# Cross attention 3's output projection and gate for its first eight token tiles, moved from the router's block into the attention's last iterations

## The reference

```
def _L1_xattn_ref(q, k, v, Wq, bq, Wk, bk, Wv, bv, Wo, bo):    # 16 heads of 16, 64 context rows
    ...
    attn = jax.nn.softmax(scores, axis=-1)
    out = jnp.einsum('bhqk,bhkd->bhqd', attn, vh)
    concat = out.transpose(0, 2, 1, 3).reshape(B, LQ, D_MODEL)
    return concat @ Wo + bo
x = x + jnp.tanh(g_xattn[1]) * _L1_xattn_ref(_layernorm(x, axis=-1), ctx_512, ctx_512, ...)
x = x + jnp.tanh(g_ffn[1]) * _L1_ffn_ref(_layernorm(x, axis=-1), ...)   # router, top 128 tokens of each of 16 experts, MLP, scatter
```

## Time and profile before

| | |
|---|---|
| median of 3 runs | 1970.08 us (1968.18 to 1970.22) |
| the profiled execution: its own time, its span | 1972.5 us, 1970.7 us |
| mean granted TensorE clock | 0.969 |
| block of cross attention 3, from the first normalisation to the last copy | 1674.0 to 1756.4 us |
| router's block up to the first MAX8 | 1757.2 to 1788.6 us |

### The profile page before, as it was taken

The page is one execution under the profiler, slowest core; times in us unless marked ns, Lnnn a source line. Parts: engine busy times, 40 slices in busy tenths (PEclk is TensorE's granted clock), DMA queues, the critical chain, the costliest instruction groups (busy, mean ns, idle before and its releaser), DMA issues. The chain is left out here.

```text
span 1970.7 us, 32332 instructions
## 1 busy us (share of the span) xinstructions
PE 1787.6 (91%) x11430; PEld 1165.9 (59%) x11430; DVE 1284.4 (65%) x2762; ACT 1034.9 (53%) x2194; POOL 693.5 (35%) x995
## 2 busy tenths in 40 slices
PE   6989999999899999998899989999999999882697
PEld 3445555555576666766567665557776555551696
DVE  5579999999724477232799973259999353878311
ACT  3479999999712345221677751147776211551232
POOL 0023333333324434242555551125556220360343
PEclk9989999999999999999899999999999999996899
DMA  3451111110000020020100002010000000037495
GB/s 123 130 172 44 44 44 44 44 44 2 2 0 1 1 60 1 1 66 0 47 5 5 4 6 71 0 47 15 7 7 6 6 0 1 17 115 185 135 321 148
DMA packets 102959, 97.23 MB, mean 49 GB/s; under 512 B 37056, under 2 KB 86544, under 8 KB 102672
## 3 DMA queue, kind: packets, MB, share of 16 engines
q1 hardware_dynamic: 99216, 90.84, 15.3%
q0 software_dynamic: 3584, 4.33, 1.2%
HBM read 78.23 MB, written 14.81 MB: 47 GB/s over the span
## 5 line engine op out<-in xcount | busy, mean ns | idle before, releaser
L613 DVE TENSOR_REDUCE negmax<-sps 128x1 f32<-128x1024 f32 x256 | 308.9, 1217 | 18.9 <-PE sps L535 14.4
L657 ACT ACTIVATE prob<-sps,negmax 128x1024 f32<-128x1024 f32 x256 | 285.5, 1116 | 25.3 <-DVE negmax L613 20.9
L1987 POOL TENSOR_TENSOR la_pr_x3kblk<-la_pr_x3kblk,la_ri 128x512 f32<-128x512 f32 x128 | 158.5, 1267 | 152.4 <-DVE la_ri L2086 152.4
L703 POOL TENSOR_TENSOR probT<-probT,after 128x128 f32<-128x128 f32 x256 | 116.9, 457 | 240.4 <-DVE probT L621 214.5
L2315 ACT ACTIVATE la_pr_x3kblk<-la_pr_x3kblk,la_nx 128x256 f32<-128x256 f32 x256 | 126.3, 494 | 100.9 <-DVE la_nx L2127 100.9
L535 PE MATMUL sps<-ks,qs 128*128 128x512 f16 x512 | 170.9, 386 | 7.6 <-PEq L42 3.1
L2537 PE MATMUL la_bs<-lf_zT,lfw 128*128 128x512 f32 x352 | 153.4, 594 | 0.0
L551 PE MATMUL tps<-ident,prob 128*128 128x128 f32 x704 | 126.1, 283 | 22.9 <-DVE probT L621 20.4
L551 PEld LDWEIGHTS tps<-ident,prob 128*128 128x128 f32 x704 | 80.6, 142 | 89.6 <-issue 44.0
L1997 POOL TENSOR_TENSOR la_qs<-la_qn,ores 128x256 f32<-128x256 f32 x128 | 97.1, 790 | 78.1 <-DVE la_qn L2143 78.1
L1614 PE MATMUL tx_s<-t_zT,tw 128*128 128x512 f32 x256 | 113.8, 593 | 1.3 <-ACT t_zT L1481 1.3
(11 more groups left out here) (384 smaller groups left out, 3867.4 us busy)
## 6 DMA issues: line engine op xcount, KB each, us to landing
w1e<-in_fc_T SPq DMA_DIRECT2D x16, 1024.0 KB, 6.2
w2e<-in_fc_T SPq DMA_DIRECT2D x16, 1024.0 KB, 9.3
qs<-q_parts SPq DMA_DIRECT2D x128, 64.0 KB, 1.9
ks<-k_parts SPq DMA_DIRECT2D x128, 64.0 KB, 1.9
q_parts<-parts SPq DMA_DIRECT2D x8, 512.0 KB, 3.6
k_parts<-parts SPq DMA_DIRECT2D x8, 512.0 KB, 3.6
tw<-in_L_xattn_a_li_w SPq DMA_DIRECT2D x4, 1024.0 KB, 8.2
lfw<-in_L_ffn_w SPq DMA_DIRECT2D x6, 640.0 KB
```

The costliest lines, as they stand in the source:

```text
L613: dve.tensor_reduce(negmax[:, n % 4:n % 4 + 1], slots[n % NS][:], X, ALU.max, negate=True).then_inc(s.max_done, 1)
L657: act.activation(prob[:, n % 3, :], slots[n % NS][:], ACT.Exp, bias=negmax[:, n % 4:n % 4 + 1], accum_out=rowsum[:, tile % 2, n % QUAD:n % ...
L703: pool.tensor_tensor(blk, blk, after[:], ALU.mult).then_inc(s.masked, 1)
L1987: ins = pool.tensor_tensor(prob[:, h:h + 2, :], prob[:, h:h + 2, :], rinv[:, h:h + 2].unsqueeze(2).to_broadcast([P, 2, 2 * P]), ALU.mult)
```

## The change

Eight of the sixteen tiles' projections leave the router's block. Inside the attention's block, TensorE gets `project_out(t)`, t = 0..7: two fp32 matmuls of 256 columns (four records in the profile), at the end of iterations 7 to 12 and, for tiles 6 and 7, ahead of `turn_probs(14, 0)` and `turn_probs(15, 0)`. They write the PSUM banks `zps` and `qps`, free by then. ScalarE gets `output_share(t)`, which copies such a bank times the gate into `share_of` (two buffers), at the end of its iterations 7 to 12, 14 and 15. GpSimd gets, at the block's start, the product gate times bias and eight additions of it to `xres` (`base`), and after `share(8)` to `share(15)` the eight additions of `share_of` (`advance`). The router's block keeps groups 2 and 3 of `project`, `base` and VectorE's addition; its statistics cover all four groups as before.

```diff
@@ cross_attention @@
-        def cross_attention(phase, H, DK, src, res, weights, context, biases, scale, ahead):
+        def cross_attention(phase, H, DK, src, res, weights, context, following, biases, scale, ahead):
...
+            wo, bo, gbo, carried, loads = following
+                share_of = sb(phase + "share", [P, 2, D], F32, c)
...
                     def _(pool):
...
+                        def base(t):
+                            pool.wait_ge(s.z_done, t + 1)
+                            pool.tensor_tensor(src(t), src(t), gbo[:], ALU.add).then_inc(s.base_done, 1)
+
+                        def advance(t):
+                            pool.wait_ge(s.base_done, t + 1)
+                            pool.wait_ge(s.w_out, t + 1)
+                            pool.tensor_tensor(src(t), src(t), share_of[:, t % 2, :], ALU.add).then_inc(s.advanced, 1)
+
+                        pool.wait_ge(s.next_in, loads)
+                        pool.tensor_scalar(gbo[:], bo[:], gate[:, 1:2], None, ALU.mult).then_inc(s.gbo_done, 1)
+                        pool.wait_ge(s.gbo_done, 1)
+                        for t in range(carried):
+                            base(t)
                         for t in range(ready, LEAD_X + AHEAD):
                             inverse_deviation(t)
                         for t in range(NT):
                             share(t)
+                            if 8 <= t < 8 + carried:
+                                advance(t - 8)
...
+                        def output_share(t):
+                            act.wait_ge(s.w_done, t + 1)
+                            if t >= 2:
+                                act.wait_ge(s.advanced, t - 1)
+                            act.activation(share_of[:, t % 2, :], (qps if t % 2 else zps)[:, 0:D], ACT.Copy,
+                                           scale=gate[:, 1:2]).then_inc(s.w_out, 1)
...
                                 queries(it + LEAD_Q)
+                            if 7 <= it < 13:
+                                output_share(it - 7)
+                            if it in (14, 15):
+                                output_share(it - 8)
...
+                        def project_out(t):
+                            if t == 0:
+                                pe.wait_ge(s.xT_done, NT)
+                                pe.wait_ge(s.next_in, loads)
+                            if t == 1:
+                                pe.wait_ge(s.qT_done, G * MC)
+                            pe.wait_ge(s.out_done, t + 1)
+                            if t >= 2:
+                                pe.wait_ge(s.w_out, t - 1)
+                            at = t % TPB * P
+                            for k in range(MC):
+                                mm = pe.matmul((qps if t % 2 else zps)[:, 0:D], res[:, t // TPB * MC + k, at:at + P], wo[:, k, :],
+                                               start=(k == 0), stop=(k == MC - 1))
+                            mm.then_inc(s.w_done, 1)
...
                                 weigh(it - 1)
+                            if 7 <= it < 13:
+                                project_out(it - 7)
...
                             weigh(t)
+                        project_out(6)
                         turn_probs(NT - 2, 0)
                         turn_probs(NT - 2, 1)
+                        project_out(7)
                         turn_probs(NT - 1, 0)
@@ router @@
+        CARRIED = 8
+        FIRST = CARRIED // J
...
-                    pool.wait_ge(s.gbo_done, 1)
-                    base(0)
+                    base(FIRST)
                     for i in range(2):
                         pool.memset(lane[i][:, 0:CAP // 2], 0.0).then_inc(s.zeroed, 1)
-                    base(1)
+                    base(FIRST + 1)
                     for g in range(G):
                         coefficients(g)
-                        if g + 2 < G:
-                            base(g + 2)
...
-                        for j in range(J):
+                        for j in range(J if g >= FIRST else 0):
...
-                    dve.tensor_scalar(gbo[:], bo[:], gate[:, 1:2], None, ALU.mult).then_inc(s.gbo_done, 1)
                     advance(0)
...
-                        if g >= 2:
-                            pe.wait_ge(s.x_done, (g - 1) * J)
...
-                    project(0)
-                    project(1)
-                    project(2)
+                    project(FIRST)
+                    project(FIRST + 1)
                     turn_rows(0)
                     for g in range(G):
                         route(g)
-                        if g == 0:
-                            project(3)
```

More of the change, by code:

```diff
@@ L739, in cross_attention @@
                 tps = ps(phase + "t_ps", [P, 512], c)
-                s = signals(phase, "@next_in @x_stats @x_moments @x_var "
+                s = signals(phase, "@next_in @gbo_done @base_done @w_done @w_out @advanced @x_stats @x_moments @x_var "
                             "@x_rstd @z_done @z_turned @xT_done @q_done @qT_done @scores @max_done @prob_ready @exp_done "
@@ L784, in _ @@
                     def _(sp):
-                        sp.wait_ge(s.next_in, ahead(sp, s.next_in))
+                        assert ahead(sp, s.next_in) == loads
+                        sp.wait_ge(s.next_in, loads)
                     @block.gpsimd
@@ L2619, in build @@
         bo = sb("r_bo", [P, D], F32, r_ctx)
+        gbo = sb("r_gbo", [P, D], F32, r_ctx)
+        CARRIED = 8
+        FIRST = CARRIED // J
+        ROUTER_LOADS = 16 * (P // (2 * D3)) + 80
         nw = sb("r_nw", [P, D], F32, r_ctx)
@@ L2636, in build @@
         cross_attention("x3", H3, D3, lambda t: xres[:, t, :], ores, x3_weights,
-                        (kblk3, vblk3, x3mo, x3var, x3rs, x3_ready), biases3, D3 ** -0.5, router_ahead)
+                        (kblk3, vblk3, x3mo, x3var, x3rs, x3_ready), (wo, bo, gbo, CARRIED, ROUTER_LOADS), biases3, D3 ** -0.5, router_ahead)
         FE = io["L1_ffn_fc1_bias"].shape[1]
@@ L2662, in build @@
         with ExitStack() as c:
-            gbo = sb("r_gbo", [P, D], F32, c)
             stat = sb("r_stat", [P, J, 6], F32, c)
@@ L2699, in build @@
             sums = p1[0][:, 0, 0:3]
-            s = signals("r", "@zeroed @base_out @gbo_done @base_done @p1_done @x_done @stats @moments @var_done "
+            s = signals("r", "@zeroed @base_out @base_done @p1_done @x_done @stats @moments @var_done "
                         "@coef_done @h_done @row_done @row_turned @xT_done @lgT_done @lgT_out @lg_turned "
@@ L2715, in _ @@
                                      row[:, g, :, 0:D]).then_inc(s.rows_out, 16)
-                    sp.wait_ge(s.x_done, G * J)
+                    sp.wait_ge(s.x_done, G * J - CARRIED)
                     sp.dma_start(out.rearrange("b (t p) c -> p (b t) c", p=P), xres[:]).then_inc(s.base_out, 16)
@@ L2755, in advance @@
                     def advance(g):
-                        for j in range(J):
+                        for j in range(J if g >= FIRST else 0):
                             t = g * J + j
-                            dve.wait_ge(s.p1_done, g * J + j // 2 * 2 + 2)
-                            dve.wait_ge(s.base_done, t + 1)
+                            dve.wait_ge(s.p1_done, t // 2 * 2 + 2 - CARRIED)
+                            dve.wait_ge(s.base_done, t + 1 - CARRIED)
                             dve.scalar_tensor_tensor(out=xres[:, t, :], in0=p1[g % 2 * 2 + j // 2][:, j % 2, :], scalar=gate[:, 1:2],
@@ L2762, in advance @@
                         for j in range(J):
-                            dve.wait_ge(s.x_done, g * J + j + 1)
+                            if g >= FIRST:
+                                dve.wait_ge(s.x_done, g * J + j + 1 - CARRIED)
                             dve.bn_stats(stat[:, j, :], xres[:, g * J + j, :]).then_inc(s.stats, 1)
@@ L3009, in _ @@
                     pe.wait_ge(s.counted, 1)
-                    pe.wait_ge(s.x_done, G * J)
+                    pe.wait_ge(s.x_done, G * J - CARRIED)
                     pe.matmul(p1[0][:, 0, 0:2], pick[:, 0:P], cnt[:], start=True, stop=True)
```

## The result

The changed kernel takes 1973.45 us (median of 20 runs, 1970.27 to 1975.88), the kernel before 1969.54 in 20 runs (1965.95 to 1971.52). The ratio is 1.0024, 95% interval 1.0018 to 1.0030: 4.7 us slower by the ratio, 3.9 by the two medians. That it is slower is clear; whether it is so by more than 0.2% is not, since the interval has 1.0020 in it. The time lies in the forecast's range. The forecast, 1972.7, was short by 0.8 us; as a difference to before it was + 2.6 against + 3.9 to + 4.7. Its inner sums are another matter, and most of this part is on them.

What follows compares the result with a forecast made beforehand. The prediction took a ring of TensorE and ScalarE to bound the attention's loop; + 7.4 (2.1 of it in the tail) - 4.8 for the router made + 2.6 on 1970.08, 1972.7 us; forecast 1971.5 to 1974.0, wider range 1969.3 to 1975.4.

Steps and rivals of the forecast that it cites:

- The loop: Attention's block, iterations 7 to 12: each projection adds its full 0.88 us, so tile 12's transposes come 5.3 us later.
- a ring without a gap: Attention's loop: TensorE and ScalarE wait on each other in turn; between `weigh` and the next transposes TensorE has no idle time.
- the costlier projections: Rival: standing alone, each projection costs 1.13 us, total + 4.6 us, 1974.7; chance 0.22, shared with a long low clock.
- the idle 0.77: TensorE's 0.77 us wait in each loop iteration, between first and second transposes while the bank is copied; said to stay.
- VectorE did not pace the loop: Rival: VectorE's 3.75 us period sets the loop, so six projections hide and only 2.1 is lost; 1967.4, chance 0.10.
- The tail: End of the attention's block, behind the loop: the last transposes come 7.4 us later, 2.1 of it lost here.
- the low clock of rows 5: Attention's tail: TensorE granted 0.59 and 0.70, mostly 1.2 GHz, so `project_out(6)` was priced at half rate, 1.77 us.
- the rival of the high clock: Rival: TensorE's clock stays high through the attention's tail; + 5.5 - 4.8 = + 0.7 us, 1970.8, chance 0.14.
- GpSimd's path: Attention's tail: `share(15)` queued behind `advance(6)` ends at 1761.05, costing nearly nothing beyond TensorE's own delay, without slack.
- Together `shift(0)` comes 4.8 us earlier: Router's block: 1.2 us from earlier rows plus 3.6 from the removed `project(3)`, a gain of 4.8 us.
- 9.2 us: Router's block: the forecast counts as wrong if `turn_rows(0)` waits for something later than 9.2 us into the block.
- everything behind `shift(0)` is as before: Router's block: last rows, logits and MAX8 keep their durations, so the whole 4.8 us gain reaches the first MAX8.

Runs made afterwards that it cites:

- the loop's part alone: The kernel before with TensorE's eight projections added at the changed kernel's places, results unused, router's block still doing all its own; ratio to before 1.0035.
- The other places: The changed kernel with projections 0 to 3 between the halves of `turn_probs`, the others ahead of `weigh(12)` and `weigh(13)`; ratio to before 0.9981.
- `share(15)` first: The changed kernel with GpSimd's `share(15)` ahead of `advance(6)` and `advance(7)`; ratio to before 1.0021.
- the router's part alone: The changed kernel without the projection, scaling and addition of the first eight tiles; ratio to before 0.9991.
- the best version: The changed kernel with projections in TensorE's idle places and all base additions in the attention's block; ratio to before 0.9973.
- the filled wait: The changed kernel with two tiles of group 3's projections done twice, to shorten TensorE's idle time ahead of `turn_rows(0)`; ratio to before 1.0021.

## Why the prediction came out as it did

**The loop: right, in mechanism and size.** Forecast 5.3, from a ring without a gap at that place; measured 5.5 (5.5 by the loop's part alone and 5.6 by the changed kernel's second profile). The price per tile was 0.92 in place of 0.88, well under the 1.04 at which the costlier projections would have decided. The other places show that the reading of the idle 0.77 was right too. VectorE's waits, which I put down to late scores, are for ScalarE's exponential; nothing hangs on it. VectorE did not pace the loop. GpSimd's product and eight additions at the block's start were free, as forecast: they are in the 0.1 by which the changed kernel's loop exceeds that of the loop's part alone.

**The tail: mis-sized, 2.1 against 0.6, by the clock alone.** From the transposes of tile 12 to the last copy it is 13.93 us in both profiles of the changed kernel and 13.33 before. The work that was added costs about what I said: 13.93 against 11.93 at the full clock on both sides, 2.0 us. But the kernel before pays 1.4 for its low clock there, and the changed one did not. I had carried the low clock of rows 5 over into the changed tail. In both profiles of the changed kernel the tail is at 2.4 GHz throughout, as the rival of the high clock said, although both waits that I had set against it are still there, 1.94 each; its 5.5 for loop and tail is nearer to the 6.2 (88.18 - 81.96) of the second profile than my 7.4. The section of the Trainium skill that I named beside it ("TensorE: Matmul & The Clock Gate", "What's actually happening": activity releases the throttle) agrees with this tail, but the profiles bear it out only as a tendency. Of seven profiles with projections behind `weigh`, six kept the clock in the tail and one, with `share(15)` first, did not; of five whose loop has no projections, four lost it and one did not; the two with the projections at other places kept it. What decides it is not shown. GpSimd's path did open, as forecast, and cost TensorE 0.69. That the first profile's attention was longer by just the forecast 7.4 is chance: 1.3 of it is in the block's first iterations, ahead of the first projection, with the clock at 0.50 for longer; the second profile of the same kernel has 0.1 there.

**The router: the failed step.** "Together `shift(0)` comes 4.8 us earlier" came out as 4.3 at full clock (the router's part alone), and as 2.6 and 4.3 in the changed kernel's two profiles; of that, 1.5 and 2.6 were left at the first MAX8. At full clock the two parts are 3.5 for `project(3)`, as forecast, and 0.8 for earlier rows in place of 1.2: GpSimd did start its additions 0.4 earlier, but they took 2.96 and 3.15 in place of 2.77, because they now run beside `r_h`. I had named 9.2 us as the point beyond which I would be wrong; it was 9.6. The sum left out what the diff does to the first `r_h`: with no additions of VectorE's own ahead of it, it falls beside GpSimd's. The Trainium skill ("SBUF — State Buffer", section "Who interferes with whom") has GpSimd and VectorE share a pair of ports that one holds for a whole instruction. The runs agree: `r_h`, with two operands in SBUF, is slowed (1.64 against 3.35), and a statistics instruction with one is not (four take 1.41 beside additions, and 1.39 without them, in the last group of the kernel before). By that section of the Trainium skill I could have foreseen it, since the diff sets the additions beside that `r_h`.

The larger miss is the clock, 1.7 to 2.8 us (28.79 and 29.91 against 27.10). My step "everything behind `shift(0)` is as before" took its durations from an execution in which the block had the full clock. The kernel before, with 64 projection records there, had it in both profiles. Of the eleven profiles with the lighter start eight have a low stretch in it, and three (the router's part alone, twice, and the best version) none. But the loop's part alone has the start of the kernel before, all 64 records, and a low stretch at its last logits too (3.27; its 32.74 against 31.39). So the heavier start does not keep the clock up by itself, and one in three against eight in eleven is too few to tell.

**The sum.** By the second profile + 6.2 - 2.6 = + 3.6, by the first + 7.4 - 1.5 = + 6.0 (7.44 - 1.48 unrounded); timed + 4.7. The forecast's + 2.6 came from a tail too dear by 1.5 and a router too generous by 2.2 to 3.3. These two errors have opposite signs, so that the time came so near is in part luck. The two parts alone, - 1.8 and + 6.9, add up to + 5.1, so they don't interact beyond what the timing tells.

What stays open: why the low stretches fall where they do. That they make the router's block longer in one execution of a program than in another is shown. That the lighter start of TensorE invites them is not: it rests on counts of profiles with one against it, and the filled wait, the one run made to test it, changed nothing that can be measured.

## What to carry to other kernels

Work that is moved into an engine's idle time must stand in the queue where that idle time is: a tile's projection cost 0.92 us behind `weigh`, and nothing one group of transposes later, in the wait for a copy. When work is taken out of a block, ask which queue its start then waits for, and which instructions of two engines fall beside each other by it; here GpSimd's order of additions and coefficients kept TensorE waiting for 2.5 us, and a better order brought `shift(0)` 1.5 us forward. And the clock's low stretches moved by as much as the terms of this sum, 1 to 4 us, so look at several profiles, and compare like clock with like, before such a term is trusted.

## What the runs showed of the hardware

- One program's executions differ by up to 8 us of 1968 (the router's part alone: 1962.37 to 1970.34), and the mean granted clock goes with them (0.973 in the shortest, 0.967 in the longest). Two profiles of it differ by 3.8 us in one block of 30, by where TensorE's stretches at 1.2 GHz fall, with the other engines' durations alike. The Trainium skill ("TensorE: Matmul & The Clock Gate", section "What's actually happening") says that the monitor runs free of the kernel's start and the transition varies from run to run. The profiles agree in so far as the low stretches of the changed kernel and of the router's part alone lie at other places from one profile to the next; those of the kernel before lay at the same place twice.
- The low clock in the attention's tail costs 1.4 to 1.6 us of some 13 (11.93 us at 2.4 GHz, 13.33 to 13.57 with it).
- A `scalar_tensor_tensor` on VectorE with two SBUF operands, 128x256, four at a time, goes from 1.64 to 3.35 us beside GpSimd's additions, and these from 2.77 to 2.96 and 3.15. With one operand in PSUM it stays at 1.65 beside additions.
- A tile's projection (four matmul records of 128x256) put alone into a ring without a gap delays it by 0.92 us, 0.04 more than in a row of 48: here standing alone among waits costs it hardly more.
